# A two-layer block on one core: B evicted straight into its PSUM bank, and both layers' token statistics on ScalarE instead of VectorE

## The reference

```python
def layer0(xn):
    s = retention(xn)                     # (q k^T * decay) v, causal
    h = silu(xn @ w1) * (xn @ w2)         # 512 wide
    h = gelu(h @ h1); h = gelu(h @ h2)
    return s, h @ w3
def layer1(xn):
    x_ssm, gate = split(xn @ W_in + b_in)
    x_conv = silu(conv4(x_ssm) + conv_b)
    B, C = split(x_conv @ W_x + b_x)      # 16 states each
    # for each token: h = A*h + x_conv[:, None]*B ; y = sum_n C*h + D*x_conv
    s = (y * silu(gate)) @ W_out + b_out
    g = xn + (rank in the upper half) * sigmoid(xn @ w_r) * ffn(xn)
    return s, g
def _layernorm(x):                        # over the 128 features of a token
    return (x - mean) / sqrt(var + eps)
```

## Time and profile before

| | us |
|---|---|
| median of 3 runs | 513.25 (510.42 to 514.96) |
| the profiled execution | 513.98 |
| its span, first to last instruction | 512.2 |
| DVE busy | 408.1 |
| PE busy | 421.7 |
| POOL busy | 391.0 |
| ACT busy | 283.2 |

### The profile page before, as it was taken

The page is one execution under the profiler, slowest core; times in us unless marked ns, Lnnn a source line. Parts: engine busy times, 40 slices in busy tenths (PEclk is TensorE's granted clock), DMA queues, the critical chain, the costliest instruction groups (busy, mean ns, idle before and its releaser), DMA issues.

```text
span 512.2 us, 6161 instructions
## 1 busy us (share of the span) xinstructions
PE 421.7 (82%) x1823; PEld 252.5 (49%) x1823; DVE 408.1 (80%) x692; ACT 283.2 (55%) x466; POOL 391.0 (76%) x317
## 2 busy tenths in 40 slices
PE   0785968897999789997999899979998998765654
PEld 0564735654565446654664467445744574321221
DVE  2174042979889998999899999998999799959985
ACT  2763663785378447764676457845775457241300
POOL 2574552898798989998899889988998799634582
PEclk9997988999999999999999999999999999896865
DMA  8400003631361318140823083215432553154320
GB/s 306 165 22 3 1 1 103 175 100 41 90 163 63 103 45 250 60 100 27 229 83 101 25 231 102 83 42 174 119 84 59 147 129 100 42 149 124 87 77 20
DMA packets 28739, 51.56 MB, mean 101 GB/s; under 512 B 3360, under 2 KB 5408, under 8 KB 28448
## 3 DMA queue, kind: packets, MB, share of 16 engines
q1 hardware_dynamic: 27696, 49.84, 33.7%
q10 hardware_dynamic: 1008, 1.29, 0.8%
HBM read 46.40 MB, written 4.72 MB: 100 GB/s over the span
## 4 chain that ended last, share of the span: by engine, by line
PE 39%; DVE 26%; issue 14%; ACT 10%; DMA 6%; POOL 3%; DVEq 1%; SPq 0%; ACTq 0%; POOLq 0%
PE bank0a L958 15%; DVE hs L1386 8%; DVE xbank L1363 8%; PE bank1a L1038 7%; PE bank0a L1080 3%; DMA Bt<-bc_rows 3%; DVE beats L1334 3%; PE ybank L1103 2%; DMA bc_rows<-bc 2%; DVE beats L1343 2%; DMA Bt<-w_in 1%; PE bank1a L1023 1%; ACT plain L678 1%; ACT xn L720 1%; DVE st L1291 1%
## 5 line engine op out<-in xcount | busy, mean ns | idle before, releaser
L582 POOL TENSOR_TENSOR hs<-hs,Ct 128x512 f32<-128x512 f32 x127 | 172.1, 1357 | 44.6 <-DVE hs L1386 25.2
L1386 DVE TENSOR_TENSOR_SCAN hs<-decay,carry,xbank 128x512 f32<-128x512 f32 x63 | 80.6, 1279 | 7.6
L1386 DVE TENSOR_TENSOR_SCAN hs<-decay,xbank 128x512 f32<-128x512 f32 x64 | 78.0, 1219 | 5.2
L544 POOL TENSOR_TENSOR hidAl<-plain,hidAh 128x512 fp32r<-128x512 f32 x48 | 67.9, 1418 | 15.5 <-ACT hidAh L679 8.9
L544 POOL TENSOR_TENSOR hidBl<-plain,hidBh 128x512 fp32r<-128x512 f32 x48 | 66.1, 1382 | 12.8 <-ACT hidBh L694 7.8
L1363 DVE TENSOR_TENSOR xbank<-xs,bbank 128x512 f32<-128x512 f32 x104 | 71.6, 688 | 3.0 <-ACT bbank L777 1.3
L678 ACT ACTIVATE plain<-bank0a,col 128x512 f32<-128x512 f32 x64 | 44.0, 688 | 38.7 <-PE bank0a L958 38.6
L958 PE MATMUL bank0a<-hidBh,hTh 128*128 128x512 f32 x128 | 55.1, 430 | 3.8 <-ACT hidAh L679 2.1
L958 PE MATMUL bank0a<-hidAh,hTh 128*128 128x512 f32 x128 | 53.8, 420 | 3.0 <-ACT q L711 1.7
L958 PE MATMUL bank0a<-hidAl,hTh 128*128 128x512 f32 x128 | 50.2, 392 | 0.0
L958 PE MATMUL bank0a<-hidBl,hTh 128*128 128x512 f32 x128 | 50.1, 392 | 0.0
(11 more groups left out here) (188 smaller groups left out, 874.8 us busy)
## 6 DMA issues: line engine op xcount, KB each, us to landing
xs<-x_rows SPq DMA_DIRECT2D x128, 256.0 KB, 3.5
xt<-x_tok SPq DMA_DIRECT2D x8, 256.0 KB, 6.1
xr<-x_feat SPq DMA_DIRECT2D x8, 256.0 KB, 7.9
x_rows<-xc SPq DMA_DIRECT2D x8, 256.0 KB, 2.0
Bt<-bc_rows SPq DMA_DIRECT2D x8, 256.0 KB, 3.4
Ct<-bc_rows SPq DMA_DIRECT2D x8, 256.0 KB, 4.6
out<-xr SPq DMA_DIRECT2D x7, 256.0 KB, 6.1
fh<-h_w SPq DMA_DIRECT2D x1, 1024.0 KB, 9.9
```

Source lines behind the costliest of these rows:

```text
L544: pool.tensor_tensor(low[:, m, :], plain[:, k % NPLAIN, :], high[:, m, :].bitcast(F32), ALU.subtract).then_inc(hidden_low, 1)
L582: pool.tensor_tensor(h, h, Ct[:, hs_(u)], ALU.mult).then_inc(p_ready, 1)
L1386: dve.tensor_tensor_scan(hs[:, i % NSTATES, :], decay[:, gr:gr + 1].broadcast_to([P, HALF]), xbank[:], 0.0 if u % 2 == 0 else carry[:, k:k ...
```

## The change

B no longer passes through DRAM. PE makes a product of its own, `W_B` (the 16 columns of B each repeated 8 times) by the convolved unit, in `bank1a` right behind the gate in slot 5, and ACT evicts it with its bias straight into `bbank` (`take_B`), behind the gate's eviction and once the last step of the unit before has read that bank. All 16 steps read `bbank`. The load Bt, `keep_B` and their semaphores go; C keeps its way through DRAM. L1_ACT gets the job "B" between "gate" and "score".

The statistics: layer 1's of all 8 units and layer 0's of units 2 to 7 leave DVE. ACT now evicts the tokens in four pieces of 128x128 that each sum into `sum1`, makes the negated mean (128x4), squares four pieces with that mean as bias, each summed into `square1`, and makes variance plus eps (128x4), all in slot 1. For layer 0 `sums_l0` stands in slot 4 and `squares_l0` in slot 5, between the eviction of B and C and that of the gate. Where POOL's `rstd` and ACT's `norm` stand is unchanged.

```diff
@@ L1_ACT
-        L1_ACT += [(_k, _n) for _k in ("xnT", "conv", "BC", "gate", "score", "score_col")]
+        L1_ACT += [(_k, _n) for _k in ("xnT", "conv", "BC", "gate", "B", "score", "score_col")]
@@ SP
-            def spread_bc(u, which):
+            def spread_c(u):
                 sp.wait_ge(bc_kept[u % 2], (u // 2 + 1) * 16)
-                if u >= 2 and which == 0:
-                    sp.wait_ge(l1_dve_full, done(L1_DVE, ("out", u - 2)))
...
                     spread_x(n, 0)
-                    spread_bc(n, 0)
                     spread_x(n, 1)
-                    spread_bc(n, 1)
+                    spread_c(n)
@@ ACT
             def to_tokens(t):
                 bank = full0(("tok", t))
-                act.activation(yn[:].rearrange("p c d -> p (c d)"), bank[:], ACT.Copy).then_inc(l0_act_done, 1)
+                for j, c in enumerate(chunks(t)):
+                    last = act.activation(yn[:, j, :], bank[:, ck(j)], ACT.Copy, accum_out=sum1[:, c:c + 1])
+                last.then_inc(l0_act_done, 1)
+
+            def squares_l1(t):
+                c = cs_(t)
+                act.wait_ge(l0_act_done, done(L0_ACT, ("tok", t)))
+                act.activation(negmean1[:, c], sum1[:, c], ACT.Copy, scale=-1.0 / P).then_inc(negmean1_ready, 1)
+                act.wait_ge(negmean1_ready, t + 1)
+                for j, c1 in enumerate(chunks(t)):
+                    last = act.activation(unused[:, j, :], yn[:, j, :], ACT.Square, bias=negmean1[:, c1:c1 + 1],
+                                          accum_out=square1[:, c1:c1 + 1])
+                last.then_inc(squared1, 1)
+                act.wait_ge(squared1, t + 1)
+                act.activation(ve1[:, c], square1[:, c], ACT.Copy, bias=EPS, scale=1.0 / P).then_inc(eps1, 1)
...
-            def keep_B(t):
-
+            def take_B(t):
                 if t > 0:
                     act.wait_ge(xb_ready, step(t, 0))
-                act.wait_ge(b_in[t % 2], (t // 2 + 1) * 16)
-                act.activation(bbank[:], Bt[:, hs_(t)], ACT.Copy).then_inc(b_kept, 1)
+                take1(("B", t), bbank[:], ACT.Identity, bias=scale("b_B"))
@@ ACT slot
                     if s == 1:
                         to_tokens(n)
+                        squares_l1(n)
...
+                if w is not None and s == 4:
+                    sums_l0(w)
                 if n is not None:
                     if s == 5:
                         convolved(n)
                         take_BC(n)
-                        take_gate(n)
+                if w is not None and s == 5:
+                    squares_l0(w)
+                if n is not None and s == 5:
+                    take_gate(n)
+                    take_B(n)
...
                         score_columns(n)
-                        keep_B(n)
@@ PE
+                def project_x(job, t, w):
+                    bank = open1a((job, t))
+                    pe.wait_ge(l1_act_done, done(L1_ACT, ("conv", t)))
+                    pe.matmul(bank[:], w, xc[:, hs_(t)], start=True, stop=True).then_inc(l1_act_full, 1)
...
                         project("gate", n, W_IN[:, P:2 * P])
+                        project_x("B", n, W_B)
@@ DVE
-                if k == 0:
-                    dve.wait_ge(b_in[u % 2], (u // 2 + 1) * 16)
-                elif k == BSTEPS:
-                    dve.wait_ge(b_kept, u + 1)
+                if k == 0:
+                    dve.wait_ge(l1_act_done, done(L1_ACT, ("B", u)))
...
-                b = Bt[:, hs_(u)] if k < BSTEPS else bbank[:]
-                dve.tensor_tensor(xbank[:], xs[:, i % NROWS, :], b, ALU.mult).then_inc(xb_ready, 1)
+                dve.tensor_tensor(xbank[:], xs[:, i % NROWS, :], bbank[:], ALU.mult).then_inc(xb_ready, 1)
...
-                    elif s == 2:
-                        stats_l1(n)
...
-                    if s == 7:
-                        stats_l0(w)
```

More of the change, by code:

```diff
@@ L80 @@
 NROWS = 5
-BSTEPS = 3
 def group_of(k):
@@ L221, in program @@
         inexact_i = sb("inexact_i", [P, 1], I32)
-        at_r = 2 * P + 2 * NSTATE
-        W_IN, W_BC, W_R, W_OUT, W_1 = (lw[:, 0:2 * P], lw[:, 2 * P:at_r], lw[:, at_r:at_r + P],
-                                       lw[:, at_r + P:at_r + 2 * P], lw[:, at_r + 2 * P:])
+        at_r = 3 * P + 2 * NSTATE
+        W_IN, W_B, W_BC, W_R, W_OUT, W_1 = (lw[:, 0:2 * P], lw[:, 2 * P:3 * P], lw[:, 3 * P:at_r], lw[:, at_r:at_r + P],
+                                            lw[:, at_r + P:at_r + 2 * P], lw[:, at_r + 2 * P:])
         xt = sb("xt", [P, CH, P])
@@ L243, in program @@
         sc = sb("sc", [P, CH, P])
+        sum0 = sb("sum0", [P, CH])
+        square0 = sb("square0", [P, CH])
+        sum1 = sb("sum1", [P, CH])
+        square1 = sb("square1", [P, CH])
+        unused = sb("unused", [P, CPH, P])
         g0 = sc[:].rearrange("p c i -> p (c i)")
@@ L341, in program @@
         l1_dve_done = sem("l1_dve_done")
-        stats1 = sem("stats1")
-        aggr1 = sem("aggr1")
+        summed0 = sem("summed0")
+        squared0 = sem("squared0")
+        summed1 = sem("summed1")
+        squared1 = sem("squared1")
         eps1 = sem("eps1")
@@ L361, in program @@
         bc_kept = [sem(f"bc_kept{i}") for i in range(2)]
-        b_in = [sem(f"b_in{i}") for i in range(2)]
         c_in = [sem(f"c_in{i}") for i in range(2)]
-        b_kept = sem("b_kept")
         xb_ready = sem("xb_ready")
@@ L429, in keep_bc @@
                 sp.dma_start(bc_rows[u % 2].rearrange("r (q t) -> q r t", q=CPH), bc[:]).then_inc(bc_kept[u % 2], 16)
-            def spread_bc(u, which):
+            def spread_c(u):
                 sp.wait_ge(bc_kept[u % 2], (u // 2 + 1) * 16)
-                if u >= 2 and which == 0:
-                    sp.wait_ge(l1_dve_full, done(L1_DVE, ("out", u - 2)))
-                rows = bc_rows[u % 2, which * NSTATE:(which + 1) * NSTATE, :].rearrange("n (o t) -> n o t", o=1)
-                sp.dma_start((Bt, Ct)[which][:, hs_(u)],
-                             rows.broadcast_to([NSTATE, DPG, HALF])).then_inc((b_in, c_in)[which][u % 2], 16)
+                rows = bc_rows[u % 2, NSTATE:2 * NSTATE, :].rearrange("n (o t) -> n o t", o=1)
+                sp.dma_start(Ct[:, hs_(u)], rows.broadcast_to([NSTATE, DPG, HALF])).then_inc(c_in[u % 2], 16)
             def spread_x(u, k):
@@ L714, in to_tokens, with sums_l0, squares_l0 @@
                 bank = full0(("tok", t))
-                act.activation(yn[:].rearrange("p c d -> p (c d)"), bank[:], ACT.Copy).then_inc(l0_act_done, 1)
+                for j, c in enumerate(chunks(t)):
[12 more added lines that the diff above has]
+                act.activation(ve1[:, c], square1[:, c], ACT.Copy, bias=EPS, scale=1.0 / P).then_inc(eps1, 1)
+            def sums_l0(t):
+                c = cs_(t)
+                act.wait_ge(x_tok_in[t % 2], (t // 2 + 1) * 16)
+                for c1 in chunks(t):
+                    last = act.activation(unused[:, c1 % CPH, :], xt[:, c1, :], ACT.Copy, accum_out=sum0[:, c1:c1 + 1])
+                last.then_inc(summed0, 1)
+                act.wait_ge(summed0, t - 1)
+                act.activation(negmean0[:, c], sum0[:, c], ACT.Copy, scale=-1.0 / P).then_inc(negmean0_ready, 1)
+            def squares_l0(t):
+                c = cs_(t)
+                act.wait_ge(negmean0_ready, t + 1)
+                for c1 in chunks(t):
+                    last = act.activation(unused[:, c1 % CPH, :], xt[:, c1, :], ACT.Square, bias=negmean0[:, c1:c1 + 1],
+                                          accum_out=square0[:, c1:c1 + 1])
+                last.then_inc(squared0, 1)
+                act.wait_ge(squared0, t - 1)
+                act.activation(ve0[:, c], square0[:, c], ACT.Copy, bias=EPS, scale=1.0 / P).then_inc(eps0, 1)
             def norm_l0(t):
@@ L1286, in residual_l0 @@
                 dve.tensor_tensor(g0[:, hs_(t)], bank0d[:], g0[:, hs_(t)], ALU.mult).then_inc(l0_dve_done, 1)
[L1288 to L1299, removed]
-                dve.tensor_scalar(ve1[:, c], mv1[:, c, 1], EPS, None, ALU.add).then_inc(eps1, 1)
-                dve.tensor_scalar(negmean1[:, c], mv1[:, c, 0], -1.0, None, ALU.mult).then_inc(negmean1_ready, 1)
             def conv_biases():
@@ L1557 @@
             "D": columns(a["L1_attn_D_param"]), "b_out": columns(a["L1_attn_b_out"]), "b1": columns(a["L1_ffn_b1"]),
-            "b2": columns(a["L1_ffn_b2"]), "b_x": np.tile(b_x, CPH).reshape(P, 1), "A_log": a_log,
+            "b2": columns(a["L1_ffn_b2"]), "b_x": np.tile(b_x, CPH).reshape(P, 1),
+            "b_B": np.repeat(b_x[:NSTATE], DPG).reshape(P, 1), "A_log": a_log,
             "gamma_col": c.pop("gamma_col")}
```

9 lines of the change are left out of this document (3 added, 6 removed).

## The result

| | before | changed |
|---|---|---|
| median us (lowest to highest) | 512.31 (510.42 to 514.96) | 525.68 (525.48 to 527.12) |
| ratio, 95% interval | | 1.0263 (1.021 to 1.0316) |
| profiled execution, its span | 513.98, 512.2 | 527.12, 525.3 |

The change makes the kernel 2.6% slower, 13.4 us. The forecast was 526.0.

The account below looks back on a forecast made before the run. The prediction took the PE and ACT chain as the bound, DVE lateness adding 0.93 us a period. Period 0 +2.2, six periods +11.2, period 7 +2.0 and tail -2.5 gave +12.9; forecast 526 us, range 512 to 538.

Parts of the forecast that it names:

- What bounds the kernel: Steady periods: PE and ACT carry the chain; DVE work outside slots 0 to 2 is worth at most 0.93 us a period.
- The statistics, layer 1: Slot 1 sums and squares on ACT delay normalisation through queues of ACT and POOL: +1.2 us a period (-0.15 to +2.0).
- The statistics, layer 0: Sums and squares fit ACT's gaps before the convolution's and gate's evictions: no cost, at most 0.3 us later gate eviction.
- Period 0: First period, with no scan beside it: layer 1's statistics delay the first convolution by 2.2 us.
- B on PE and ACT: Slot 5: B's product waits for the gate's eviction, h1 +2.0 us (0.9 to 2.3); B's copy leaving slot 8 gives -0.4.
- The floor of 52.42: Length in us of a steady period where DVE adds no wait; the added terms were predicted to make it 55.22.
- period 7: Last convolution interval, no z work on ACT: +0.4 us for the normalisation, +2.0 with B and its copy.
- the tail: Last unit, where DVE sets the end: B there earlier and a shorter step 2 give -2.5 us (-1.1 to -5.0).
- rival 4: Last unit: B comes early, but x's rows hide it; inside the tail's bound, no separate chance given.
- Rival 1: The wait that goes was the bound: late periods fall to 52.42 and the tail shortens, 8 us gained, 505; chance 0.15.
- Rival 2: ACT's sums ride along and most of the loss is B's alone: 515 us, no change; chance 0.13.
- Rival 3: TensorE's clock also falls each period as the later normalisation leaves PE less busy: another 10 us, 536; chance 0.10.

Follow-up runs that it names:

- B alone: Changed kernel with both layers' statistics back on DVE and tokens evicted in one piece; 519.02 us, ratio 1.0103 to the kernel before.
- B late: Changed kernel with B's product and eviction behind h1's first tile, both layers' statistics on DVE; 506.7 us, ratio 0.9897 to the kernel before.
- B late with layer 0's statistics: Changed kernel with B's product and eviction behind h1's first tile, only layer 1's statistics back on DVE; 509.49 us, ratio 0.9924 to the kernel before.

## Why the prediction was right

The time, the sign and both mechanisms came out. Step by step:

**What bounds the kernel.** Right. The kernel with layer 0's statistics alone on ACT shows it most plainly: DVE lighter, no change. And the chain of before goes through DVE from slot 8 on in the long periods alone, as I had read it from their lengths.

**The statistics, layer 1.** Right in kind, too large in size. I took 0.17 for a sum, between 0 and 0.27. Groups of the kernel after by line and shape (busy us, mean ns of one):

```profile
L723 ACT ACTIVATE unused<-yn,negmean 128x128 f32<-128x128 f32 x32 | 12.5, 390 | 0.3
...
L714 ACT ACTIVATE yn<-bank0a 128x128 f32<-128x128 f32 x32 | 8.4, 280 | 2.5 <-PE bank0a L1044 2.4
...
L714 ACT ACTIVATION_READ_ACCUMULATOR yn<-bank0a 128x1 f32 x32 | 6.8, 212 | 0.0
```

A read takes 0.19 to 0.21 but overlaps. Token pieces follow each other at 0.25 and squares at 0.39, against 0.18 and 0.28 of my walk without sums: 0.07 and 0.11 a sum, if that walk, an estimate, is right. The 128x4 instructions took 0.21, not 0.17. So the variance was there 3.30 us behind the tokens, not 3.8, and the normalisation 1.35 later than before, not 1.95. I had the term at +1.2, and the convolution starts 9.83 behind the first token piece (352.99 - 343.16) against 9.27 (341.36 - 332.09): +0.56. The mis-sized step is the cost of a sum. Behind it the walk holds as it stands: from POOL's power to the normalisation 1.33 us (349.62 - 348.29), as I had it, and from there to ynT 2.65 us (352.27 - 349.62), my 1.55 + 1.1. I also sized the term on one kind of period only. Before, the convolution came 9.27 behind the tokens in every second period and 8.97 in the others, and now it is 9.83 in both: +0.56 and +0.86, 0.7 on average. The route, through the copy of z tile 1 and POOL's rest of it, was right; moving POOL's power showed that the route was the cost, since the same sums then cost nothing. The constant-scale formula that I quoted from the Trainium skill ("ScalarE: Activation LUTs", What ACT_TABLE_LOAD costs) gives 293 ns for 128 elements and 386 with one per-partition operand; the rows say 280 and 390, so they agree to 13 ns. The advice of the Trainium skill (same page, Rules for kernel authors) to leave adds and multiplies to VectorE came out right in the order of the changed kernel (5.2 to 7.2 us) and made no difference once POOL's power stood first (507.1 against 506.7).

**The statistics, layer 0.** Costed at nothing, measured at nothing within 0.5% beside B through DRAM. Beside B's early product it was not measured alone. Period 0 is an exception: there the chain holds the squares from 86.22 for 1.55 us, with the gate's eviction behind them.

**B on PE and ACT.** Predicted +2.0, measured +1.9 to +1.95. Right, for the reason given. One bound was too narrow: "the product alone, 0.9, if PE had other work for the wait (it has none in order)". With h1's first tile there it has, and the cost falls below my lower bound of 0.9, to 0.16. The copy of B I had at -0.4; the kernel with B alone leaves -0.1 to -0.2 for it (periods of 54.15 to 54.22 are 1.7 to 1.8 above 52.42, where the product costs 1.9).

**The floor of 52.42.** With the measured parts, 52.42 + 0.56 + 1.9 - 0.1 = 54.78 is what the shorter periods took (54.77 twice). With +0.86 for the other kind it is 55.08, and those took 54.98 to 55.05. The first took 56.23: mean 55.14 against 55.22. In the first the squares are on the chain and the clock was lower: the granted clock in the 6 us from its first tap was 0.50, and 0.63 before, and matmuls three to eight of that convolution took 4.84 against 3.85. So my oversized terms, 0.5 for the statistics and 0.1 for the product, were balanced by 0.3 too much taken off for the copy and by 0.2 a period for the long first one. The sum was right to 0.1 us a period by more luck than its working shows.

**Period 0, period 7, the tail.** +2.2 predicted and read, but only 1.8 of it is the walk (10.06 us from the first token piece to the first tap, against 8.30). The rest is when the tokens came, 67.14 against 66.70, and over all traces that varies from 65.9 to 68.9. So the first tap came at 74.2 to 76.0 with layer 1's statistics on DVE, and at 76.1 to 79.0 with them on ACT and POOL unmoved, and a single trace is good to about 1.5 there. Period 7: normalisation at 4.71 us against 4.73, predicted 5.1; the interval +2.1, predicted +2.0. The tail -2.0 against -2.5: B was there in time, and x's rows then held step 0, which was rival 4.

**The rivals.** Rival 1 (DVE was the bound, 505): false for this kernel, but its gain was there to be had and hidden by B's product. Freed of that, B in its bank reached 506.7. I had written that it "needs B's product and the squares both under cover", and with B's product under cover it is what came. Rival 2 (sums ride along, 515): false as a whole; sums cost less than I took, but their queue cost remained. Rival 3 (clock): not in the changed kernel, which has full clock from the second convolution to the last and the 0.72 of before behind that:

```profile
353.00:408.00 55.00, 50.59 (x224) 29.94 (x226) 45.37 (x63) 39.78 (x92) 46.32 (x39) 1.00 0.37 97
...
459.00:465.00 6.00, 6.00 (x15) 3.08 (x16) 3.74 (x6) 0.40 (x1) 3.63 (x3) 0.72 0.01 1
```

The clock did fall in one or two periods of three other kernels (B alone, B late, B late with layer 0's statistics), where the normalisation stands 5.0 to 5.1 us behind the tokens as before. So what the rival made it depend on, a late normalisation, is not what did it.

**What stays open.** The long periods of before have Bt's load and then DVE's list on their chain, and they are gone where Bt is gone and the product is late. Whether it was Bt's arrival or the slow steps that read it was not tried apart. Nor was it settled whether layer 0's statistics on ACT cost 0 or 3 us beside the late B, or what decides in which periods the clock falls.

## What to carry to other kernels

Before moving work to a less busy engine, read what stands behind it in that engine's order, and who waits for that: here the added 3.3 us on ACT cost through one POOL instruction queued behind a copy, and moving a single call undid it. When a new product needs a bank that was just filled, put an independent product between the two, best where PE already waits for something; that one place was worth 12 us, with the statistics on DVE (519.0 to 506.7) and on ACT (525.7 to 513.9). Read the chain period by period: the average of before hid that every second one went through DVE and a load. And undo each half of a change alone: the half that looked like the loss, B, held the gain.

## What the runs showed of the hardware

A summed ACTIVATE leaves a second row, ACTIVATION_READ_ACCUMULATOR, of 187 to 212 ns, which mostly overlaps its neighbours: summed pieces of 128x128 followed each other at 0.25 us with a constant scale and at 0.39 with one per-partition operand. That is 0.07 and 0.11 us more than my estimate for pieces without a sum, which no run has. ACT's eviction from one bank into another took 0.66 us, against 0.69 into SBUF. And PE's granted clock could not be told from its busy time alone. In the kernel with B late and the statistics on DVE, PE was busy 4.16 us of the 6 from 224.95 and 4.15 of the 6 from 331.44, both at the same place ahead of a convolution: the clock was 1.00 in the first and 0.76 in the second. In the changed kernel it was busy 3.82 of 6 at that place (from 346.19), with 1.00.
